# Causal attention of 16 heads of 64: order of scores and weighings, and a ring of five for the probabilities

## The reference

```python
def _L3_xattn_ref(q, k, v, Wq, Wk, Wv, Wo):          # q: layernorm(x); k, v: the context
    query = jnp.einsum('bse,hed->bhsd', q, Wq)       # KEY_DIM = VALUE_DIM = 64, 16 heads
    key_p = jnp.einsum('bse,hed->bhsd', k, Wk)
    value = jnp.einsum('bse,hed->bhsd', v, Wv)
    scores = jnp.einsum('bhqd,bhkd->bhqk', query, key_p) / jnp.sqrt(jnp.asarray(KEY_DIM, jnp.float32))
    causal = jnp.tril(jnp.ones((S, S), dtype=scores.dtype))
    scores = scores + (1.0 - causal) * NEG
    alphas = jax.nn.softmax(scores, axis=-1)
    attention = jnp.einsum('bhqk,bhkd->bhqd', alphas, value)
    attention = attention.reshape(B, S, NUM_HEADS * VALUE_DIM)
    return jnp.einsum('bsf,fe->bse', attention, Wo)
```

## Time and profile before

| | |
|---|---|
| median of 3 runs | 2100.21 us (2098.96 to 2108.5) |
| profiled execution, its own time | 2091.46 us |
| its span | 2089.7 us |
| mean granted clock of TensorE over the span | 0.858 |
| TensorE busy in the span | 1607.8 us (77%) |
| VectorE, ScalarE, GpSimd busy | 996.2, 674.8, 512.9 us |

### The profile page before, as it was taken

How to read it: one execution, slowest core, us unless ns; L and a number is a source line. 1 busy time by engine, 2 the same in 40 slices (tenths; PEclk the granted TensorE clock), 3 DMA queues, 4 the chain that set the end, 5 groups by cost and what they waited for, 6 DMA issues and landing times. The chain is left out here.

```text
span 2089.7 us, 33375 instructions
## 1 busy us (share of the span) xinstructions
PE 1607.8 (77%) x12250; PEld 1235.2 (59%) x12250; DVE 996.2 (48%) x2190; ACT 674.8 (32%) x1408; POOL 512.9 (25%) x583
## 2 busy tenths in 40 slices
PE   4898775905888519981699746888699999999976
PEld 2565654804566418871466434655478888888766
DVE  2675262524454422113366446776426554455542
ACT  1464342302555101111366413434332222222111
POOL 2110043052444020005331064431042223222110
PEclk8798797957999659995799967988799999999986
DMA  4230553435644258852756034442110000000001
GB/s 135 68 83 18 185 213 105 135 91 153 141 112 92 75 204 295 301 197 86 166 130 133 3 85 108 103 92 53 44 55 7 6 7 1 6 6 2 1 7 41
DMA packets 89430, 195.54 MB, mean 94 GB/s; under 512 B 13536, under 2 KB 62176, under 8 KB 80704
## 3 DMA queue, kind: packets, MB, share of 16 engines
q1 hardware_dynamic: 76352, 173.07, 28.9%
q0 software_dynamic: 4608, 12.59, 1.8%
q10 hardware_dynamic: 8320, 7.87, 1.1%
HBM read 136.47 MB, written 57.02 MB: 93 GB/s over the span
## 5 line engine op out<-in xcount | busy, mean ns | idle before, releaser
L806 DVE TENSOR_REDUCE a_sb_mx<-a_mx 128x2 f32<-128x512 f32 x256 | 164.8, 686 | 97.7 <-PE a_mx L634 97.4
L1161 DVE RECIPROCAL a_sb_rden<-a_ot 128x256 f32<-128x256 f32 x64 | 112.1, 1752 | 146.6 <-PE a_ot L1047 146.5
L558 ACT ACTIVATE a_sb_probs<-a_ex 128x512 f32<-128x512 f32 x256 | 139.2, 598 | 103.9 <-PE a_ex L655 103.3
L230 PE MATMUL a_gp<-g_ident,a_sb_xn 128*128 128x128 f32 x128 | 25.1, 329 | 163.0 <-POOL a_sb_xn L206 80.0
L230 PEld LDWEIGHTS a_gp<-g_ident,a_sb_xn 128*128 128x128 f32 x128 | 16.9, 165 | 167.5 <-DMA a_sb_bo<-a_bo 70.9
L806 DVE TENSOR_REDUCE f_sb_mx<-f_mx 128x2 f32<-128x512 f32 x128 | 82.2, 684 | 36.7 <-PE f_mx L634 36.3
L558 ACT ACTIVATE f_sb_probs<-f_ex 128x512 f32<-128x512 f32 x128 | 69.5, 597 | 71.5 <-PE f_ex L655 71.4
L990 ACT ACTIVATE a_sb_probs<-a_sc 128x512 f32<-128x512 f32 x64 | 38.2, 597 | 167.9 <-PE a_sc L1035 111.7
L959 POOL TENSOR_SCALAR_AFFINE_SELECT a_sb_probs<-a_sb_probs 128x256 f32<-128x256 f32 x128 | 49.2, 409 | 164.9 <-ACT a_sb_probs L991 164.8
L655 PE MATMUL a_ex<-a_sb_QP,a_sb_KP 49*128 49x256 f32 x512 | 68.1, 343 | 24.8 <-ACT a_sb_probs L558 21.3
L952 POOL TENSOR_TENSOR a_sb_q_lo<-a_sb_whole,a_sb_q_hi 128x512 fp32r<-128x512 f32 x32 | 40.7, 1271 | 180.0 <-ACT a_sb_q_hi L981 180.0
(11 more groups left out here) (427 smaller groups left out, 3929.5 us busy)
## 6 DMA issues: line engine op xcount, KB each, us to landing
f_sb_wb<-f_w SPq DMA_DIRECT2D x20, 2052.0 KB, 11.3
a_sb_kvT<-ctxT SPq DMA_DIRECT2D x32, 256.0 KB, 3.5
a_q_moved<-a_sb_qs SPq DMA_DIRECT2D x16, 512.0 KB, 3.5
a_sb_QP<-a_q_moved SPq DMA_DIRECT2D x32, 256.0 KB, 4.7
f_x_slots<-f_sb_zero SPq DMA_DIRECT2D x1, 6144.0 KB, 20.1
f_sb_xs<-f_x_slots SPq DMA_DIRECT2D x20, 256.0 KB, 2.8
f_y_slots<-f_sb_ys ACTq DMA_DIRECT2D x20, 256.0 KB, 2.6
a_sb_QP<-a_q_moved SPq DMA_DIRECT2D x32, 128.0 KB, 5.0
```

The source lines that it names most:

```text
L230: op = pe.transpose(out[:, k, t * P:(t + 1) * P], xn[:, t, k * P:(k + 1) * P], g.ident[:])
L558: act.activation(probs[:, group % 3, 2 * (u % 2) + par], EX[par][:], ACT.Exp, scale=scale)\
L806: dve.tensor_reduce(mx[:, :, column(2 * u + par)], MX[par][:], AX.X, ALU.max, negate=True)\
L1161: dve.reciprocal(rden[:, n], OT[n][:, 1, :])
```

## The change

weigh6 and weigh7 move from the start of the following step to the end of their own (their lag goes from 2 to 1). Scores stand in two runs of four in place of four runs of two. Each of weigh0 to weigh6 stands behind a projection: k1, k2, k3, v0 and v1, v2, v3; weigh7 stands right behind weigh6. The ring of the probabilities goes from three to five buffers. Number, size and operands of all instructions are as before.

```diff
--- before.py
+++ after.py
@@ -843,14 +843,16 @@
             dve.drain()
 
 
-WIDE_ORDER = [("max0", 1), ("max1", 1), ("weigh6", 2), ("weigh7", 2), ("xT", 0),
-              ("max2", 1), ("max3", 1), ("q0", 0), ("q1", 0),
+WIDE_ORDER = [("max0", 1), ("max1", 1), ("xT", 0), ("max2", 1), ("max3", 1), ("q0", 0), ("q1", 0),
               ("max4", 1), ("max5", 1), ("neg0", 1), ("y", 2),
               ("max6", 1), ("max7", 1), ("q2", 0), ("q3", 0), ("k0", 0), ("neg1", 1),
-              ("score0", 1), ("score1", 1), ("k1", 0), ("k2", 0),
-              ("score2", 1), ("score3", 1), ("weigh0", 1), ("k3", 0), ("weigh1", 1),
-              ("score4", 1), ("score5", 1), ("weigh2", 1), ("v0", 0), ("weigh3", 1), ("v1", 0),
-              ("score6", 1), ("score7", 1), ("weigh4", 1), ("v2", 0), ("norm", -1), ("weigh5", 1), ("v3", 0)]
+              ("score0", 1), ("score1", 1), ("score2", 1), ("score3", 1),
+              ("k1", 0), ("weigh0", 1), ("k2", 0), ("weigh1", 1), ("k3", 0), ("weigh2", 1), ("v0", 0), ("weigh3", 1),
+              ("score4", 1), ("score5", 1), ("score6", 1), ("score7", 1),
+              ("v1", 0), ("weigh4", 1), ("v2", 0), ("weigh5", 1), ("norm", -1), ("v3", 0), ("weigh6", 1), ("weigh7", 1)]
+
+
+PROBS = 5
 
 
 def attention64(nc, g, name, w):
@@ -864,7 +866,7 @@
     gp = Ring([u for u in flat if u[0] in small], 2)
     scr = Ring([u for u in flat if u[0].startswith(("max", "score"))], 2)
     otr = Ring([u for u in flat if u[0].startswith("weigh")], 2)
-    prr = Ring([u for u in flat if u[0].startswith("score")], 3)
+    prr = Ring([u for u in flat if u[0].startswith("score")], PROBS)
     lor = Ring([u for u in flat if u[0] in small and u[0][0] in "qk"], 2)
 
     with ExitStack() as ctx:
@@ -888,7 +890,7 @@
         ones = sb("ones", [P, hd])
         mx = sb("mx", [P, TT, H])
         negT = sb("negT", [P, 2, S], F32R)
-        probs = sb("probs", [P, 3, 2, TT, S])
+        probs = sb("probs", [P, PROBS, 2, TT, S])
         rden = sb("rden", [P, 2, S])
         oT = sb("oT", [P, C, S])
         GP = [ctx.enter_context(nc.psum_tensor(f"{name}_gp{i}", [P, 2, S], F32)) for i in range(2)]
@@ -983,8 +985,8 @@
                     elif what.startswith("score"):
                         u, pair, n = (what, b), scr.slot((what, b)), prr.slot((what, b))
                         k = prr.place[u]
-                        if k >= 3:
-                            free_of = f"weigh{(k - 3) % 8}", (k - 3) // 8
+                        if k >= PROBS:
+                            free_of = f"weigh{(k - PROBS) % 8}", (k - PROBS) // 8
                             done(act, ot_full, otr, free_of)
                         done(act, sc_full, scr, u)
                         act.activation(probs[:, n, :, 0, :], SC[pair][:, :, 0, :], ACT.Exp, scale=scale)
```

## The result

The changed kernel takes 2167.53 us (median of 4 runs, 2162.93 to 2171.65) against 2102.89 us for the kernel before, run beside it: a ratio of 1.0305, 95% interval 1.0268 to 1.0342, so 64.6 us slower. The forecast was slower, by 29 us, with a range that ended at 2142 us.

The account below looks back on a forecast made before the run. The prediction took TensorE, its matmuls busy for the whole 60.90 us step, to set the length of a step. It summed 0.8 + 16.0 + 12.4 + 0 = +29.2 us to forecast 2129 us, range 2112 to 2142.

Parts of the forecast that it names:

- TensorE's own work: On TensorE in seven steps, only neighbours of units change: net +0.11 us a step, +0.8 us in all.
- The rule of the Trainium skill on tiling modes: A change of tiling mode drains TensorE; counted so, one change fewer a step, -1.3 us in place of +0.8.
- The longer run of scores: At score2 and score3, TensorE would not wait for ScalarE to read earlier scores: cost nothing.
- the slack of 0.56 us: Time between ScalarE's second exponential of score0 ending and score1 ending, so score2 need not wait.
- weigh6 and weigh7 ahead of max0: At max2, TensorE stalls because VectorE reads max0 late: 2.66 us a step, six new times, 16.0 us.
- the 0.19 at max3: After the 2.47 us stall at max2, max3 waits 0.19 us more for VectorE to read max1.
- The clock after the stall: TensorE's clock drops behind 4 of the 6 new stalls, 3.1 us lost each: 12.4 us, bounds 0 and 18.6.
- two of three: Share of stalls taken to lower TensorE's clock, from the earlier trace's three gaps: 4 of 6.
- The ends: First and last steps of the stage: 0, with 4 us either way for one clock drop more or fewer.
- Rival 4: Clock stays down longer after each of six stalls, some 6 us each: 2153 us; chance 0.05.
- Rivals 2 and 3: 2: no stall at max2, 2101 us, chance 0.11. 3: faster, last step loses its gap, 2086 us, chance 0.06.
- rival 1: The stall at max2 comes but TensorE's clock does not fall: +16.8, 2117 us; chance 0.16.

Follow-up runs that it names:

- e1: Changed kernel with weigh6 and weigh7 put back behind max1 of the following step; runs of four scores and ring of five stay: 2134.48 us against 2100.72.
- e8: Against the kernel before: no two scores side by side, ring of five, weigh6 behind max1 and weigh7 behind max3 of the next step: 2088.10 us against 2098.49.
- e2: Kernel before with only weigh6 and weigh7 moved to the end of their own step; scores in pairs, ring of three: 2131.03 us against 2100.72.
- e9: e1 with weigh0 put between score2 and score3 and weigh4 between score6 and score7: 2137.62 us against 2103.27 for the kernel before.
- e4: Order of e1, but scores in runs of three, three and two: 2114.91 us against 2100.72 for the kernel before.
- e3: Kernel before with five buffers for the probabilities in place of three, nothing else: 2097.36 us against 2100.72.
- e10: Kernel before with weigh7 alone moved from behind max1 to behind max3; ring of three, scores in pairs: 2101.34 us against 2103.27.

## Why the prediction was wrong

The sum had four terms, 0.8, 16.0, 12.4 and 0 for the ends; the longer run of scores stood at nothing.

- **TensorE's own work, +0.8.** Right as far as it can be seen: 0.11 a step closes the account of the step above. The rule of the Trainium skill on tiling modes (TensorEngine Tiling (Array Packing), Key Properties) would have moved the sum by 2.1 us, and no run here can tell that.
- **The longer run of scores, "Cost nothing".** This step failed, with +33.8 us (e1), over half of the whole. The reasoning looked at what score2 waits for, the slack of 0.56 us, which held: no stall at score2 appears. It did not ask what 6.4 us of scores alone do to the clock. The trace of before had a hint that I didn't read: two of its steps were 62.6 us long in place of 60.9, both with k1 and k2 behind a pair at half clock in part, 5.34 us from start to start in place of 3.65:

```profile
1620.29 5.41 PE L999 MATMUL a_gp<-a_sb_kvT,a_sb_wk 128*128 128x256 f32 x16
1625.63 0.39 PE L1031 MATMUL a_sc<-a_sb_q_hi,a_sb_k_hi 64*128 64x256 f32 x2
```

The 13.3 us at 0.51 in the last step may be another, but every kernel here has such a stretch, of 10 to 17 us, behind the 2.1 us gap, e8 with its single scores in the steps too, so it doesn't tell the scores from the gap. As a rival, a fall with TensorE busy was missing.

- **weigh6 and weigh7 ahead of max0, +16.0.** Right in mechanism: seven waits, six of them new, at the unit named, 2.42 each against 2.47; without the 0.19 at max3 the six come to 14.5 us. The reading that TensorE's matmuls waited long only three times, all at the end, left out the stage's start, where they waited 7.8 us for the first norm and 2.4 for a weight; both are as before.
- **The clock after the stall, +12.4.** Right in kind, too small in size. Each of the new stalls lowered the clock, not two of three: behind the six, max2 to q1 took 6.58 to 8.11 us in place of 5.03, 15.6 us together. With the stalls that makes 30.1 us in the changed kernel, against 28.4 forecast. That e2 alone measured +30.3 is in part luck: there max2 to q1 took 6.88 us at most behind a stall, 1.9 lost against up to 3.1, and the remainder are falls at pairs.
- **The ends, 0.** As far as it can be told apart: from the seventh y to the eighth it is 51.9 us in place of 49.8, within the 4 us allowed.

Rival 4, 2153 us, had too much half clock behind the stalls; its sum came nearer for a reason that it didn't give. Rivals 2 and 3 fell with the seven waits, rival 1 with the half clock behind each. The range failed since all its bounds were bounds of the terms that I had.

## What to carry to other kernels

Where TensorE sets the time, a reordering has to be checked for two things besides waits: which engine reads a bank first after the move (here 4.6 us of VectorE work ahead of the one reduction that TensorE needs), and which kinds of matmul come to stand side by side, since the clock can halve with TensorE busy all along. Count the half-clock stretches of a step before and name the unit ahead of each. Put dense projections between units that go with such stretches, and let as few of them as possible stand side by side; a weighing in between did not serve here (e9, 34.4 us lost, as with the uncut four).

## What the runs showed of the hardware that I had not expected

- A fully busy TensorE was put to 1.2 GHz 12 times out of 12 in or behind four score units side by side (e1), 8 times out of 12 at runs of three (e4), 2 to 4 times out of 24 at pairs without the stall (before, e3, e10), and at none of 48 singles (e8), all over six steps.
- About 1 us of extra dense matmuls in the middle of such a run saved what it cost or more, whether as matmuls of 128 rows (20 us of half clock in place of 72, 18 us added, no time lost against e1) or as overlapping pairs of 64 rows (41 us, 15 us added, 2120 us in place of 2134).
- A stall of TensorE of only 2.3 to 2.4 us brought half clock each of the six times, from within it or right behind it, in the changed kernel as in e2.
- Falls can repeat in place from step to step: e2 had four steps of 68.22 to 68.23 us, each with the same three half-clock stretches, though its separate runs differ by 27 us. Why is open.
